# A product of users in float32 becomes three in the rounded type, and so do the small counting products

## The reference, cut to what matters

```
h = item_feat @ W_item.T + b_item                       # 10000 x 128
b = layernorm(x) @ W_user.T + b_user                    # 10000 x 128
x = x + relu(adj @ h + b)                               # adj is 10000 x 10000, float32
logits = layernorm(x) @ gate_w + gate_b                 # 8 experts
idx, prb = argmax(softmax(logits)), its probability
pos = how many earlier users chose the same expert      # cumsum of the one-hot rows
kept = pos < 1563
x = x + (relu(x' @ w1[idx] + b1) @ w2[idx] + b2) * prb * kept    # x' = layernorm(x)
```

## Time and profile before

| what | value |
|---|---|
| median of 3 runs | 1382.54 us (1380.58 to 1383.38) |
| the profiled execution, its own time | 1382.88 us |
| its span, first to last instruction | 1381.1 us, so 1.8 us lie around the span |
| mean granted clock of PE | 0.984 |
| PE busy | 1339.5 us (97%) |
| DVE busy | 1169.4 us (85%) |
| ACT busy | 945.8 us (68%) |
| POOL busy | 576.0 us (42%) |
| blocks 0 to 19 | about 14 to 1167 us |
| experts | from there to 1381 us |

### The profile page before, as it was taken

The page is one execution under the profiler, slowest core; times in us unless marked ns, Lnnn a source line. Parts: engine busy times, 40 slices in busy tenths (PEclk is TensorE's granted clock), DMA queues, the critical chain, the costliest instruction groups (busy, mean ns, idle before and its releaser), DMA issues. The chain is left out here.

```text
span 1381.1 us, 19857 instructions
## 1 busy us (share of the span) xinstructions
PE 1339.5 (97%) x6152; PEld 1097.9 (79%) x6152; DVE 1169.4 (85%) x1781; ACT 945.8 (68%) x906; POOL 576.0 (42%) x335
## 2 busy tenths in 40 slices
PE   7999999999999999999999999999999999899993
PEld 6888888888888888888888888888888877677772
DVE  6999989899898898988989989889898894577774
ACT  5777767767667677676776767767767664677871
POOL 0001154262450633605426145162360563588887
PEclk9999999999999999999999999999999999899997
DMA  8999999999999999999999999999999985233220
GB/s 327 359 379 405 412 397 373 372 370 379 367 367 377 359 379 369 366 384 360 375 375 366 380 364 372 372 363 372 378 363 376 366 302 162 80 100 100 71 49 3
DMA packets 99950, 441.56 MB, mean 320 GB/s; under 512 B 29635, under 2 KB 37867, under 8 KB 99905
## 3 DMA queue, kind: packets, MB, share of 16 engines
q1 hardware_dynamic: 69017, 418.17, 80.3%
q0 software_dynamic: 24928, 12.59, 3.8%
q10 hardware_dynamic: 5960, 10.24, 2.3%
HBM read 428.11 MB, written 23.87 MB: 327 GB/s over the span
## 5 line engine op out<-in xcount | busy, mean ns | idle before, releaser
L694 DVE TENSOR_TENSOR a_lo<-raw,a_hi 128x2000 fp32r<-128x2000 f32 (+1 forms) x400 | 867.7, 2189 | 101.4 <-ACT a_hi L501 96.7
L501 ACT CAST a_hi<-raw 128x2000 fp32r<-128x2000 f32 (+1 forms) x400 | 724.8, 1826 | 287.1 <-PE bank L1109 189.5
L1107 PE MATMUL bank<-a_hi,h_hi 128*128 128x500 f32 x1560 | 622.7, 399 | 0.6 <-ACT a_hi L501 0.6
L1109 PE MATMUL bank<-a_hi,h_lo 128*128 128x500 f32 x1560 | 607.5, 389 | 0.0
L1118 PE MATMUL bank<-a_lo,h_hi 128*128 128x500 f32 x1560 | 419.0, 389 | 0.0
L1107 PEld LDWEIGHTS bank<-a_hi,h_hi 128*128 128x128 f32 x1560 | 294.3, 189 | 63.2 <-issue 5.7
L1109 PEld LDWEIGHTS bank<-a_hi,h_lo 128*128 128x128 f32 x1560 | 294.9, 189 | 60.5 <-issue 4.4
L1118 PEld LDWEIGHTS bank<-a_lo,h_hi 128*128 128x128 f32 x1560 | 293.9, 188 | 59.6
L1003 POOL TENSOR_TENSOR late<-ve,neghalf 125x4 f32<-125x4 f32 x20 | 55.3, 2763 | 597.5 <-DVE ve L711 597.5
L1011 POOL DMA_INDIRECT records<-late,slot x80 | 170.3, 2129 | 22.8 <-issue 22.8
L1075 POOL DMA_INDIRECT out<-raw x104 | 144.4, 1388 | 43.9 <-issue 33.6
(11 more groups left out here) (128 smaller groups left out, 848.0 us busy)
## 6 DMA issues: line engine op xcount, KB each, us to landing
raw<-adj_m SPq DMA_DIRECT2D x380, 1000.0 KB, 6.5
raw<-adj_m SPq DMA_DIRECT2D x20, 500.0 KB
xT<-x_t ACTq DMA_DIRECT2D x20, 250.0 KB, 4.2
late<-items_t SPq DMA_DIRECT2D x19, 256.0 KB, 4.5
raw<-records SPq DMA_DIRECT2D x24, 191.8 KB
xb<-x ACTq DMA_DIRECT2D x20, 224.0 KB
raw<-w SPq DMA_DIRECT2D x8, 258.5 KB
raw<-w SPq DMA_DIRECT2D x8, 256.0 KB
```

What stands on the lines that cost most here:

```text
L501: last = nc.scalar.copy(a_hi[:, g % HI_RING, 0:m], raw[:, g % RAW, 0:m])
L694: last = v.tensor_tensor(a_lo[:, g % RAW, 0:m], raw[:, g % RAW, 0:m], a_hi[:, g % HI_RING, 0:m].bitcast(F32), ALU.subtract)
L1107: nc.tensor.matmul(acc[q][:, 0:BLOCK], h_hi[:, k * HID:(k + 1) * HID], a, start=(k == 0), stop=False)
L1109: last = nc.tensor.matmul(acc[q][:, 0:BLOCK], h_lo[:, k * HID:(k + 1) * HID], a, start=False, stop=False)
```

## The change

The users' product is now made of three products in float32r, in the same place of the same accumulation. `take_xl` writes the high part `xlT_hi` (where `colsT` lies). DVE gets a new step at g=12, `xl_low`, which subtracts it from PSUM into `xlT_lo` (where `rows` lies). The weights are split once at the start, by ACT (`w_user_hi`) and DVE (`w_user_lo`, over the constants). The counting products take `tri`, `run` and `counts` in float32r; their numbers are small whole numbers. The 125 x 125 ones become one column, `one_r`, read 125 times by its access pattern.

```
+            def xl_low(b):
+                dve.wait_ge(xlT_ready, b + 1)
+                v.tensor_tensor(xlT_lo[:, :], ps_x[:, 0:BLOCK], xlT_hi[:, :].bitcast(F32),
+                                ALU.subtract).then_inc(xlT_lo_ready, 1)
...
+                    if g == 12:
+                        xl_low(b)
...
             def normalize_x(b):
...
-                    act.wait_ge(xl_turned, b)
+                    act.wait_ge(users_done, b)
...
-                nc.scalar.copy(colsT[:, :], ps_x[:, 0:BLOCK]).then_inc(xlT_ready, 1)
+                nc.scalar.copy(xlT_hi[:, :], ps_x[:, 0:BLOCK]).then_inc(xlT_ready, 1)
...
             act.wait_ge(consts_loaded, 32)
+            nc.scalar.copy(w_user_hi[:, :], const("w_user")).then_inc(w_user_hi_ready, 1)
...
-            v.memset(ones[:, :], 1.0).then_inc(set_up, 1)
-            v.memset(counts[:, :], 0.0).then_inc(set_up, 1)
+            v.memset(one[:, :], 1.0).then_inc(set_up, 1)
             v.memset(neghalf[:, :], -0.5).then_inc(set_up, 1)
             dve.wait_ge(consts_loaded, 32)
             v.tensor_copy(tok[:, :, :].rearrange("p a j -> p (a j)"), const("tok", TP)).then_inc(set_up, 1)
+            v.tensor_scalar(counts[:, :], const("gate_b", TP)[:, 0:EXPERTS], 0.0, None, ALU.mult).then_inc(set_up, 1)
+            v.tensor_copy(tri[:, :], const("tri", TP)).then_inc(set_up, 1)
+            dve.wait_ge(set_up, 1)
+            v.tensor_copy(one_r[:, :], one[:, :]).then_inc(set_up, 1)
+            dve.wait_ge(w_user_hi_ready, 1)
+            v.tensor_tensor(w_user_lo[:, :], const("w_user"), w_user_hi[:, :].bitcast(F32),
+                            ALU.subtract).then_inc(w_user_lo_ready, 1)
...
             def turn_x(b):
...
-                    pe.wait_ge(xlT_ready, b)
+                    pe.wait_ge(xlT_lo_ready, b)
...
             def users(b, q):
-                pe.wait_ge(xlT_ready, b + 1)
-                nc.tensor.matmul(acc[q][:, 0:BLOCK], const("w_user"), colsT[:, :], start=False,
+                pe.wait_ge(xlT_lo_ready, b + 1)
+                nc.tensor.matmul(acc[q][:, 0:BLOCK], w_user_hi[:, :], xlT_hi[:, :], start=False, stop=False)
+                nc.tensor.matmul(acc[q][:, 0:BLOCK], w_user_lo[:, :], xlT_hi[:, :], start=False, stop=False)
+                nc.tensor.matmul(acc[q][:, 0:BLOCK], w_user_hi[:, :], xlT_lo[:, :], start=False,
                                  stop=False).then_inc(users_done, 1)
...
-                nc.tensor.matmul(ps_count, const("tri", TP), run[:, 3, :], start=True, stop=False)
-                nc.tensor.matmul(ps_count, ones[:, :], counts[:, :], start=False, stop=True).then_inc(count_done, 1)
+                nc.tensor.matmul(ps_count, tri[:, :], run[:, 3, :], start=True, stop=False)
+                nc.tensor.matmul(ps_count, ones, counts[:, :], start=False, stop=True).then_inc(count_done, 1)
```

More of the change, by code:

```diff
@@ L74 @@
 _at = 0
-for _name, _n in (("ident", 128), ("tri", TP), ("rev", TILES * EXPERTS), ("tok", 2 * TILES),
-                  ("w_user", HID), ("gate_w", EXPERTS), ("gate_b", TILES * EXPERTS),
+for _name, _n in (("ident", 128), ("w_user", HID), ("tri", TP), ("rev", TILES * EXPERTS), ("tok", 2 * TILES),
+                  ("gate_w", EXPERTS), ("gate_b", TILES * EXPERTS),
                   ("run_at", 1), ("run_no", EXPERTS), ("edge_of", EXPERTS),
@@ L113, in build @@
         xT = sb("xT", [128, BLOCK])
+        rows_at = -(-nc.sbuf_base // 32) * 32
         rows = sb("rows", [TP, TILES, HID])
+        xlT_lo = nc.alloc_sbuf_tensor_at("xlT_lo", [128, BLOCK], F32R, offset=rows_at)
+        cols_at = -(-nc.sbuf_base // 32) * 32
         colsT = sb("colsT", [128, BLOCK])
+        xlT_hi = nc.alloc_sbuf_tensor_at("xlT_hi", [128, BLOCK], F32R, offset=cols_at)
         gnn = sb("gnn", [128, BLOCK])
@@ L120, in build @@
         items = late[:, 0:2 * GMAX * HID].rearrange("p (r n) -> p r n", r=2)
-        ones = sb("ones", [TP, TP])
-        counts = sb("counts", [TP, EXPERTS])
+        one = sb("one", [TP, 2])
+        one_r = sb("one_r", [TP, 2], F32R)
+        ones = one_r[:, 0:1].broadcast_to([TP, TP])
+        counts = sb("counts", [TP, EXPERTS], F32R)
         neghalf = sb("neghalf", [TP, TILES])
@@ L141, in build @@
         oh = sb("oh", [TP, TILES, EXPERTS])
-        run = sb("run", [TP, TILES, EXPERTS])
+        run = sb("run", [TP, TILES, EXPERTS], F32R)
         place = sb("place", [TP, TILES, EXPERTS])
@@ L240, in build @@
         xlT_ready = sem("xlT_ready")
+        xlT_lo_ready = sem("xlT_lo_ready")
+        w_user_hi_ready = sem("w_user_hi_ready")
+        w_user_lo_ready = sem("w_user_lo_ready")
         users_done = sem("users_done")
@@ L357, in wait_on_pool @@
             pool.wait_ge(s, n)
-            return nc.gpsimd.tensor_tensor(carrier_pool[:, cell:cell + 1], ones[:, 0:1], ones[:, 0:1], ALU.add)
+            return nc.gpsimd.tensor_tensor(carrier_pool[:, cell:cell + 1], one[:, 0:1], one[:, 0:1], ALU.add)
         block = ctx.enter_context(nc.Block())
@@ L765, in pick @@
                 chain.link(v.tensor_tensor(run[:, 1, :], oh[:, 0, :], oh[:, 1, :], ALU.add))
-                chain.link(v.tensor_tensor(run[:, 2, :], run[:, 1, :], oh[:, 2, :], ALU.add))
-                v.tensor_tensor(run[:, 3, :], run[:, 2, :], oh[:, 3, :], ALU.add).then_inc(run_ready, 1)
+                chain.link(v.tensor_tensor(run[:, 2, :], run[:, 1, :].bitcast(F32), oh[:, 2, :], ALU.add))
+                v.tensor_tensor(run[:, 3, :], run[:, 2, :].bitcast(F32), oh[:, 3, :], ALU.add).then_inc(run_ready, 1)
             def find_unused():
@@ L835, in assign @@
                 dve.wait_ge(run_ready, n + 1)
-                chain.link(v.tensor_tensor(place[:, :, :], run[:, :, :],
+                chain.link(v.tensor_tensor(place[:, :, :], run[:, :, :].bitcast(F32),
                                            ps_count.unsqueeze(1).broadcast_to([TP, TILES, EXPERTS]), ALU.add))
@@ L844, in settle @@
                                           ALU.mult, ALU.add))
-                chain.did(v.tensor_tensor(counts[:, :], counts[:, :], run[:, 3, :], ALU.add))
+                chain.did(v.tensor_tensor(counts[:, :], counts[:, :].bitcast(F32), run[:, 3, :].bitcast(F32), ALU.add))
                 dve.wait_ge(exp_done, n + 1)
@@ L1062, in body @@
                     x_scale(b + 1)
-            pool.wait_ge(set_up, 6)
+            pool.wait_ge(set_up, 8)
             x_scale(0)
@@ L1165, in count @@
                 pe.wait_ge(run_ready, m + 1)
-                nc.tensor.matmul(ps_count, const("tri", TP), run[:, 3, :], start=True, stop=False)
-                nc.tensor.matmul(ps_count, ones[:, :], counts[:, :], start=False, stop=True).then_inc(count_done, 1)
+                nc.tensor.matmul(ps_count, tri[:, :], run[:, 3, :], start=True, stop=False)
+                nc.tensor.matmul(ps_count, ones, counts[:, :], start=False, stop=True).then_inc(count_done, 1)
             def total(m):
                 pe.wait_ge(run_ready, m + 1)
-                nc.tensor.matmul(ps_total, ones[:, :], run[:, 3, :], start=True, stop=False)
-                nc.tensor.matmul(ps_total, ones[:, :], counts[:, :], start=False, stop=True).then_inc(total_done, 1)
+                nc.tensor.matmul(ps_total, ones, run[:, 3, :], start=True, stop=False)
+                nc.tensor.matmul(ps_total, ones, counts[:, :], start=False, stop=True).then_inc(total_done, 1)
             def body(i, q):
```

11 lines of the change are left out of this document (8 added, 3 removed).

## The result

The changed kernel takes 1373.73 us (median of 5 runs, 1369.9 to 1377.12), the kernel before 1382.54 beside it (5 runs, 1380.58 to 1384.44). The ratio is 0.9933, 95% interval 0.9907 to 0.996. The unchanged kernel after, run again in the experiments, gave 1373.04 us (6 runs) against 1381.91 (23 runs): 0.994, 0.9916 to 0.9964. So the gain is 8.8 us by the first pair and 8.9 by the second, where 6.3 was forecast against the median. The direction was right and the forecast gain too small: 1373.73 lies at the lower edge of the range (1373.5 to 1381), and the ratio applied to 1382.54 gives 1373.3, just outside it.

What follows compares the result with a forecast made beforehand. PE was taken to bound blocks 0 to 18. Savings of 7.0 us there and 0.4 at the last count, less 0.9 at the start, gave -6.5 us: 1376.4, stated as 1376.2 against the median, range 1373.5 to 1381.

Steps and rivals of the forecast that it cites:

- PE bounds blocks 0 to 18, and a microsecond taken from it there is one off the run: Blocks 0 to 18: a microsecond off PE shortens the run by one, off DVE by nothing; a block takes 56.79 us.
- The users' product, 3 x 0.226 for 0.84: Each block: three rounded products take 0.68 us instead of 0.84, saving 0.16 a block, 3.0 us over 19.
- The counts, half of 0.44: Counting products: two MATMULs for four, 0.22 us saved a count, 4.0 us over 17 counts and one total.
- DVE's step costs nothing: `xl_low` at g=12, 0.67 us 20 times, is covered by DVE's lead of 8 us over PE; cost nothing.
- The start, +0.9 us: Before PE's first product: four new instructions among DVE's small tensors cost 0.9 us, between 0.4 and 2.2.
- gives nothing back: Start: ACT's first h copy, freed of the table load, gains nothing, as items and their product hold PE until 14.1.
- The last count, -0.4: Block 19, on the chain at clock 0.50: the last count takes 0.86 us, of which half, 0.4 us, goes.
- Block 19 adds nothing: Block 19: PE's savings there are worth nothing, as POOL's zeros land at 1158.93 behind its own queue and the loads.
- B: Rival: transfers take PE's place, savings return as ACT's wait for `raw`; +0.9 us at most, 1383 us; 8%.
- D: Rival: users' product and counts both save their upper bounds, 10 us in all, 1373 us; 11%.

Runs made afterwards that it cites:

- the run with the subtractions in blocks 0 to 18: Changed kernel plus three extra 128x448 DVE subtractions into an unread bank at g=12 of blocks 0 to 18, not block 19: 1374.5 us, ratio 0.9953.
- the light start: Changed kernel with the memset of `colsT` and centring of `gate_w` first on DVE, PE's two waits moved behind the first h products: 1372.24 us, ratio 0.9926.
- the run with three more subtractions: Changed kernel plus three extra 128x448 DVE subtractions into an unread bank at g=12 of each block, ahead of `xl_low`: 1370.81 us, ratio 0.9925.

## Where the prediction held, and the step that failed

- **PE bounds blocks 0 to 18, and a microsecond taken from it there is one off the run**: right. From the last product of block 1 to that of block 18 it is 956.5 us in the three profiles of the kernel before and 949.4 in the two of the changed one. That is 7.1 us for 17 blocks. The prediction's block of 56.79 us was misread: it is a mean that takes in the 66.7 us of block 19. The steady block was 56.24, and is 55.83 where 56.4 was forecast.
- **The users' product, 3 x 0.226 for 0.84**: right, 0.69 by the starts; 0.18 a block when done alone, for 0.16.
- **The counts, half of 0.44**: right, 0.21; 0.25 a block when done alone, for 0.22. Both terms were some 10% too small: from block 2 to block 18 they came to 7.1 us, where the sum has 17 x 0.38 + 0.22 = 6.7 with the one `total`, which lies in block 18. What the further 0.03 us a block is, the starts of the products don't show.
- **DVE's step costs nothing**: right, nobody waits for `xlT_lo`, and 2 us more in the same place are still covered.
- **The start, +0.9 us**: this is the step that failed. The last product of block 0 stands at 87.6 and 87.4 us in the changed kernel and at 87.8, 88.0 and 86.9 before; with the 0.16 that the users' product saves in it, the start cost some 0.1 us by these, and 0.3 if the two further profiles with the same start are taken in (87.3 and 88.5); the scatter of about 1 us is as large as the forecast term. Two errors met. First, I took one operation's full start-to-start time for each new instruction. In a row of small independent ones the next starts much sooner:

```profile
5.45 0.17 DVE L932 COPY tok<-cst 125x8 f32<-125x8 f32 x1 [4.54 <-DMA gnn<-item_consts]
5.53 0.17 DVE L933 TENSOR_SCALAR counts<-cst 125x8 fp32r<-125x8 f32 x1
5.60 0.22 DVE L934 CAST tri<-cst 125x125 fp32r<-125x125 f32 x1
5.74 0.16 DVE L936 CAST one_r<-one 125x2 fp32r<-125x2 f32 x1
5.81 0.29 DVE L938 TENSOR_TENSOR w_user_lo<-cst,w_user_hi 128x128 fp32r<-128x128 f32 x1
```

That is DVE's timeline of the changed kernel. The first product came 0.5 us later than before (7.00 for 6.49), not 0.9. Second, the prediction says that freeing ACT of the table load "gives nothing back". ACT's timeline of the changed kernel:

```profile
1.89 1.28 ACT L586 ACT_TABLE_LOAD   x1 [1.89 <-issue]
...
10.74 0.62 ACT L500 CAST h_hi<-h_raw 128x512 fp32r<-128x512 f32 x1 [4.99 <-DVE h_raw L686]
11.26 1.85 ACT L514 CAST a_hi<-raw 128x2000 fp32r<-128x2000 f32 x1
```

Before, the first copy of `a_hi` stood behind the load of 10.28 us and began at 12.10, so it ended at 13.95 and PE could start its first big product at 14.10. Now it ends at 13.11, and only the h product holds PE, until 14.34. So 0.24 us of the 0.5 was left at that point (0.4 in the second profile, 14.57). The third profile of the kernel before, and the run with the subtractions in blocks 0 to 18, whose start is the changed kernel's, show it more plainly, as their h products are fast (1.16 us for eight, where the first profiles have 2.07 and 2.08):

```profile
14.11 0.47 PE L1107 MATMUL bank<-a_hi,h_hi 128*128 128x500 f32 x1 [0.83 <-ACT a_hi L501]
```

```profile
13.62 0.48 PE L1145 MATMUL bank<-a_hi,h_hi 128*128 128x500 f32 x1
```

Before, PE waited 0.83 us for ACT's copy, behind the table load; now that wait is gone, and the first big product comes 0.5 us earlier although the first product of all came later. So the ACT path, which the prediction put at nothing, gives back what the new instructions cost.
- **The last count, -0.4**: right, 0.86 us became 1173.15 - 1172.71 = 0.44.
- **Block 19 adds nothing**: PE's savings there did add nothing, as POOL's landed zeros hold the end. But the chain through block 19 changed all the same, by -1.6 and +1.3 us, together with the length of the half-clock stretch and the time that the zeros take to land. The prediction took both as fixed and gave them no term. The second is 19.1 to 22.7 us over the 14 profiles and 19.1 to 21.2 in the three of the kernel before alone; whether the change lengthens it is not shown.

Put together: up to `x1_scale` -7.3 for the forecast's -6.1. Of the 1.2 between them some 0.75 is there by the end of block 1, which is the start's mis-sized term, and 0.45 comes in the next 17 blocks (7.1 for 6.7). Behind it -1.1 for -0.4, of which -0.4 is the last count, and the clock and the landing lie in the rest. So 7.3 + 0.4 = 7.7 us can be put down to the change, give or take the scatter of the start. The further 0.7 of the profiles, and 1.1 of the medians, lie in terms that vary from one execution to the next by up to 4 us; whether the change leans on them was not settled.

Of the rivals B falls too: ACT waits for no transfer in 800 us though the rate rose from 375 to 378 GB/s. D gave nearly the time that was measured (1373), but by terms that were not the cause: that it came so near is luck.

No version was shown to beat the changed kernel: the intervals of the light start (0.9898 to 0.9954) and of the changed kernel (0.9916 to 0.9964) overlap, and so does that of the run with three more subtractions (0.991 to 0.994).

## What to carry to other kernels

A float32 product inside a chain of rounded ones can be traded for three rounded ones at a gain of 0.16 to 0.18 us at 500 columns, and a small float32 product for a rounded one at half its time, where the engine that makes the low part has slack. At a start, ask for each instruction what else ends just before the instant that it delays; an added delay and a removed one may meet there and cancel. Where the end hangs on transfers and on the granted clock, cut the profile into stretches at instants of the chain, and take several profiles of both kernels before a difference in such a stretch is put down to the change.

## What the runs showed of the hardware

- The table load of ACT ran at 1.89 us, ahead of the wait for the constants that holds its first copy (5.45), and cost nothing there. Before it ran at 10.28 us, between DVE's h and the copy of it, and in the third profile PE waited 0.83 us for the copies behind it.
- A 125 x 125 weight tensor read from a single column by a repeated read takes 250 ns for a product of 8 columns, a full one 255, and the block is 55.99 us with either.
- Small DVE operations that need nothing of each other start 0.07 to 0.08 us apart though each is shown 0.17 long; behind the cast of 125 x 125 it is 0.14.
- The stretches at 1.2 GHz near the last counts added up to 6.8 or 13.7 us from one execution of the kernel before to the next, and over all 14 profiles, of all kernels, to 0 to 13.7. Behind a PE standstill of 2.84 us there followed 3.4 or 6.8 us, and the longer went with 1.5 us more on POOL's chain.
- POOL's first issue of zeros took 1.4 us where DVE's low part had ended before it, and 2.2 to 2.4 where it still ran, with its end 1.25 to 1.26 us behind that of the low part: in 8 and 6 profiles, without exception.
